# Row maxima of masked attention scores: the mask of half of the score banks is added by the vector engine instead of by a matmul

## The reference

```python
q, k, v = X @ Wq.T + bq, ctx @ Wk.T + bk, ctx @ Wv.T + bv      # 32 query heads of 8, 8 groups of keys and values
scores = einsum('bgrqd,bgkd->bgrqk', q, k) / sqrt(8)
scores = where(causal_mask | padding_mask, -inf, scores)
w = softmax(scores, axis=-1)
x = x + tanh(g_xattn) * ((w @ v) @ Wo.T + bo)                  # X is layernorm(x)
x = x + tanh(g_ffn) * moe(layernorm(x))                        # top 2 of 16 experts, silu(g) * u, 96 wide
```

## Time and profile before

| what | value |
|---|---|
| runs of the kernel before | 242.26 us, median of 3 (242.17 to 242.55) |
| the profiled execution, its own time | 242.28 us |
| its span, first to last instruction | 240.5 us |
| PE, DVE, ACT, POOL busy | 220.8, 170.2, 96.7, 94.8 us |

### The profile page before, as it was taken

The page is one execution under the profiler, slowest core; times in us unless marked ns, Lnnn a source line. Parts: engine busy times, 40 slices in busy tenths (PEclk is TensorE's granted clock), DMA queues, the critical chain, the costliest instruction groups (busy, mean ns, idle before and its releaser), DMA issues.

```text
span 240.5 us, 3821 instructions
## 1 busy us (share of the span) xinstructions
PE 220.8 (92%) x1279; PEld 159.1 (66%) x1279; DVE 170.2 (71%) x355; ACT 96.7 (40%) x190; POOL 94.8 (39%) x127
## 2 busy tenths in 40 slices
PE   0688798989999999999999899999999899999993
PEld 0675563565555555546466778879898798888892
DVE  2578978658777878785832678659984888774665
ACT  2456358756676767665776210110101111011000
POOL 6239325400608393937301021307996363320000
PEclk9999999999999999999999999999999999999998
DMA  6372320008761202020203100042546222123105
GB/s 186 102 235 57 78 55 22 4 0 180 170 149 29 60 8 67 1 65 9 59 8 131 46 0 0 5 140 64 147 114 189 94 87 81 52 46 88 44 0 174
DMA packets 26274, 18.33 MB, mean 76 GB/s; under 512 B 15600, under 2 KB 22320, under 8 KB 26256
## 3 DMA queue, kind: packets, MB, share of 16 engines
q1 hardware_dynamic: 25952, 17.87, 27.4%
q10 hardware_dynamic: 304, 0.22, 0.4%
HBM read 14.15 MB, written 1.11 MB: 63 GB/s over the span
## 4 chain that ended last, share of the span: by engine, by line
PE 70%; DVE 9%; POOL 7%; DMA 5%; ACT 3%; issue 3%; SPq 1%; ACTq 0%; DVEq 0%; POOLq 0%
PE bank L1019 64%; DMA wkv_n<-in_L_xattn_Wv 2%; DVE mneg L879 2%; POOL cT L551 2%; POOL w_d L555 2%; DMA w_t<-comb_d 2%; PE bank L1079 2%; POOL cT L550 2%; DVE pT L947 1%; POOL w_d L554 1%; ACT q L616 1%; DVE x_sb L1012 1%; DMA q<-q 1%; DVE q L953 1%; PE bank L1059 1%
## 5 line engine op out<-in xcount | busy, mean ns | idle before, releaser
L1019 PE MATMUL bank<-xT,cT 128*128 128x512 f32 x288 | 70.7, 393 | 1.0 <-DVE pT L939 0.7
L1019 PEld LDWEIGHTS bank<-xT,cT 128*128 128x128 f32 x288 | 52.6, 188 | 12.4 <-issue 1.2
L879 DVE TENSOR_REDUCE mneg<-bank 128x4 f32<-128x512 f32 x64 | 43.0, 684 | 11.6 <-PE bank L1019 10.6
L683 ACT ACTIVATE pT<-bank 128x512 f32<-128x512 f32 x24 | 14.4, 599 | 78.5 <-PE bank L1019 78.5
L696 ACT ACTIVATE pT<-bank 128x512 f32<-128x512 f32 x64 | 37.9, 599 | 18.8 <-PE bank L1019 17.8
L1019 PE MATMUL bank<-w_d,q 128*128 128x256 f32 x288 | 38.6, 284 | 1.7 <-issue 0.9
L1019 PEld LDWEIGHTS bank<-w_d,q 128*128 128x128 f32 x288 | 37.0, 190 | 4.5 <-issue 3.1
L1019 PE MATMUL bank<-q,kz 112*128 112x512 f32 x64 | 37.5, 586 | 0.0
L1019 PE MATMUL bank<-kz,q 96*128 96x512 f32 x64 | 26.5, 420 | 2.4 <-DVE mneg L879 1.8
L939 DVE TENSOR_TENSOR pT<-pT,bank 128x512 f32<-128x512 f32 x24 | 16.4, 684 | 17.1 <-PE bank L1019 15.2
L1019 PE MATMUL bank<-ident_b,cmask 128*128 128x512 bf16 x64 | 24.5, 383 | 1.2 <-ACT pT L696 0.6
(11 more groups left out here) (127 smaller groups left out, 278.3 us busy)
## 6 DMA issues: line engine op xcount, KB each, us to landing
w_t<-comb_d SPq DMA_DIRECT2D x16, 192.0 KB, 2.8
w_t<-comb_d SPq DMA_DIRECT2D x16, 128.0 KB, 2.9
padf<-in_L_ffn_down_w SPq DMA_DIRECT2D x12, 128.0 KB, 2.3
c_sb<-in_ctx SPq DMA_DIRECT2D x2, 512.0 KB, 6.5
q<-cT SPq DMA_DIRECT2D x8, 128.0 KB, 2.4
w_t<-comb_d SPq DMA_DIRECT2D x16, 64.0 KB, 2.7
out<-x_sb SPq DMA_DIRECT2D x4, 256.0 KB, 2.4
c_sb<-in_L_ffn_gate_w SPq DMA_DIRECT2D x8, 96.0 KB, 2.1
```

What stands on the lines that cost most here:

```text
L683: nc.scalar.activation(act_g[:, n % 2], bank[0][:], ACT.Silu).then_inc(a_ok, 1)
L879: nc.vector.tensor_reduce(mneg[:, r, 4 * hf:4 * hf + 4], bank[SQ_BANK[n % 3]][:].rearrange("p (g k) -> p g k", g=4), X, ALU.max, negate=Tr ...
L1019: return nc.tensor.matmul(dst, a, b, start=start, stop=stop, skip_group_check=True)
```

## The change

For the banks with odd `n` from 8 to 63 (half of the groups of batches 1 to 7, 28 banks) the mask matmul of the first pass goes. The matmul of queries and keys then ends the bank by itself and signals `s_done`. In its place `row_max` issues four fused operations on DVE, one for each group of 128 keys: each adds the scores in PSUM and `cmask` in SBUF, multiplies by -1, writes the 128 results to a new scratch tile `masked`, and keeps their minimum, which is the negated maximum, in `mneg`. The other 36 banks, and the whole second pass, are as before.

```diff
+        masked = sb("masked", [P, 4, L])
...
+        def added_by_reduction(n):
+
+            return bool(n % 2 and G <= n < CH)
...
             ve.wait_ge(s_done, n + 1)
             if n >= G:
                 ve.wait_ge(m_parts, n // G)
+            if added_by_reduction(n):
+                ve.wait_ge(max_ok, n - 1)
+                for g in range(4):
+                    ins = nc.vector.tensor_tensor_reduce(masked[:, g], bank[SQ_BANK[n % 3]][:, g * L:(g + 1) * L], cmask[:, n // G],
+                                                         -1.0, 4.0 * BIG, ALU.add, ALU.min, mneg[:, r, 4 * hf + g:4 * hf + g + 1])
+                ins.then_inc(max_ok, 1)
+                return
             nc.vector.tensor_reduce(mneg[:, r, 4 * hf:4 * hf + 4], ...
...
-            mm(ps[:], q4[...], kz[...], True, False)
+            bare = added_by_reduction(n)
+            ins = mm(ps[:], q4[...], kz[...], True, bare)
+            if bare:
+                ins.then_inc(s_done, 1)
+                return
             mm(ps[:], ident_b[:], cmask[:, b].unsqueeze(1).to_broadcast([P, 4, L]), False, True).then_inc(s_done, 1)
```

More of the change, by code:

```diff
@@ L1129, in scores_q @@
                 s, g4, ps = b % KZ, slice(4 * hf, 4 * hf + 4), bank[SQ_BANK[n % 3]]
-                mm(ps[:], q4[0:3 * QR, hf, r, toks(b)], kz[0:3 * QR, s, g4].rearrange("p g k -> p (g k)"), True, False)
+                bare = added_by_reduction(n)
+                ins = mm(ps[:], q4[0:3 * QR, hf, r, toks(b)], kz[0:3 * QR, s, g4].rearrange("p g k -> p (g k)"), True, bare)
+                if bare:
+                    ins.then_inc(s_done, 1)
+                    return
                 mm(ps[:], ident_b[:], cmask[:, b].unsqueeze(1).to_broadcast([P, 4, L]), False, True).then_inc(s_done, 1)
```

## The result

The changed kernel takes 240.29 us (median of 7 runs, 239.95 to 241.83) against 242.25 before (7 runs, 242.11 to 242.55). The ratio is 0.9925, 95% interval 0.9902 to 0.9947. The forecast was 243.0 us, slower; the measured time lies in its range, 239.0 to 253.0, and the direction is the other one, near rival 1's 239.8. The profiled execution took 239.97 us.

A forecast was written before the change was run, and what follows sets the result against it. PE bounds the kernel, and DVE takes over at nearly the same length. Opening +1.6, second piece -0.5, four full batches 0, last piece -0.4 sum to +0.7 us on 242.28: 243.0 us, range 239.0 to 253.0.

The forecast's parts named there:

- rival 1: POOL's stalls of `max_parts` go, up to 0.97 us a batch, and banks may cost less: 239.8 us; chance 0.28.
- PE's saving, 0.23 us a matmul: One mask matmul goes in each of 28 banks: 6.4 us in all on PE, 0.9 us a batch.
- PE alone would need only 10.5 us: Length of a full batch if PE alone bound it, against 11.4 to 11.6 us busy before.
- DVE's price of a bank, 1.12 us: Four overlapping pairs of fused operation and write replace a 0.60 us reduction: 0.52 us more a bank, 14.6 for 28.
- The opening, +1.6: Four banks before `max_parts` of batch 1: 2.1 us more on DVE, less its 0.48 us wait for ACT.
- Full batches even at 1.12 us a bank: Four full batches: DVE needs 2.1 us more where 1.9, 2.7, 2.1 and 2.1 are free, so 0 us.
- The 0.6 us of the second batch will be eaten: Second full batch: its -0.6 us is lost to waits that two engines near 100% give each other.
- the pairs under 0.25 us: Sign that the forecast is wrong: pairs of fused operation and write on DVE take under 0.25 us.
- the short `max_parts`: Sign of POOL's stalls going: `max_parts` short, beside batches of 10.5 to 10.9 us with PE still full.
- Rival 2: Fused operations on DVE don't overlap, 1.44 us a bank: +8.3 us, 250.6; chance 0.24, and 0.06 toward 1.77.
- Rival 3: POOL delays each of 112 fused operations by 0.138 us: 15 us more on DVE; chance 0.04.
- The clock stays at its upper level: PE's clock is granted as 1.00 also in pieces where PE has short waits.

The follow-up runs named there:

- pe_only: Changed kernel with the mask left out of the maxima of the 28 banks, so PE has its saving and DVE its old load; 238.8 us.
- from_batch2: Changed kernel with the change for the odd banks of batches 2 to 7 alone, 24 banks; 0.6 us faster than the changed kernel by the medians.
- bank_1_12_f2: Changed kernel with four one-column copies added to each fused bank, for batches 2 to 7 alone; at the upper end of 239.9 to 240.5 us.
- pool_pieces: Changed kernel with POOL's 512-column splits of the first four tiles' gate and up weights cut in four; within 0.4 us of the changed kernel.
- bank_1_12: Changed kernel with four idle one-column copies from PSUM added to each fused bank, which then takes 1.10 us; 242.93 us.
- all_from2: Changed kernel with all banks of batches 2 to 7 by fused operations and batch 1 the old way; 2.1 us below all_groups' median.
- all_groups: Changed kernel with all 56 banks of batches 1 to 7 by fused operations, two scratch tiles in turn; median 240.1 us.

## Why the prediction was wrong, step by step

- **PE's saving, 0.23 us a matmul: right.** Slots with a bare bank are 0.20 to 0.24 us shorter. With PE alone relieved (pe_only) the time falls by 3.4 us, of the 6.4 that 28 matmuls are worth. "PE alone would need only 10.5 us" a batch was wrong: it needs 10.71, because `TO` waits for ACT.
- **DVE's price of a bank, 1.12 us: wrong, and enough to turn the forecast's sign.** It measures 0.84, close to the lower end (0.82). I added 0.075 us for the write of each minimum, the pace of the shortest instructions; it costs almost nothing, since the next fused operation starts with it. The extra is 0.24 us a bank, 6.8 for all, and not 14.6. In the same sum, with 1.0 us more a batch where 1.9 to 2.7 are free, DVE is not the bound of the full batches: 0.5 - 0.5 - 4 x 0.9 - 0.4 is -4.0 us, 238.3. That is faster, and by 2 us too much: it lacks `TO`'s wait for ACT, in all four batches, and the wait behind POOL's stall, in two.
- **The opening, +1.6: right in kind, +0.74 in size.** By the same rule and the measured price it is 4 x 0.24 - 0.48 = 0.5. from_batch2 shows it from the other side: its opening is 0.72 us shorter.
- **Full batches even at 1.12 us a bank: wrong too.** bank_1_12_f2 has them 1.7 us shorter, -0.62, -0.67, -0.20 and -0.20. With this step right the forecast would have been 241.3 us, faster even at 1.12 us a bank. In the last two batches its picture nearly holds: DVE is busy for 10.92 of 11.18 us; its busy time grew by 1.9 us, not by 2.1. In the second its own arithmetic had given -0.6, and that came whole. In the first DVE's busy time grew by only 0.83 us (9.56 to 10.39), not by 2.1; that the engines run ahead of each other by up to three banks, so that a piece of DVE's work falls in another piece of the table, may be the reason, but no run shows it.
- **"The 0.6 us of the second batch will be eaten": wrong.** That piece has pe_only's length, 10.70 to 10.74 us, in every version with only the odd banks bare. The waits that were to eat it (PE can lead by three banks only) did not come.
- **Rival 1** had the time (239.8), and that was luck: it is the middle of two sums, both with a bank's cost too high (1.12 and 0.95 us) and with stalls that go. Its mechanism was wrong. `max_parts` did not leave POOL's way, because DVE's waits between the statistics and `max_parts` took up the added work, and PE's shorter slots drew it nearer (from 83.50, the aggregate, to 89.08 are 5.58 us, where it was 5.98 before), and the stalls grew. They cost 0.24 us in each of two batches (pool_pieces). Of its signs the pairs under 0.25 us and the full PE came, and the short `max_parts` did not.
- **Rival 2**, no overlap, 1.28 to 1.44 us a bank: excluded by the timeline. The estimate from the Trainium skill's figures (VectorE: DVE Perf Modes, the section on the TRN2 errata) was 1.28 us a bank, with 258 ns for an operation of 128 columns from PSUM. The trace does not agree: an operation takes 284 ns by its row, and the next one starts 211 ns after it. Another page of the Trainium skill (Vector Engine (DVE) Microarchitecture Reference, section 5.2) gives about 75 ns an instruction after overlap and 1.04 ns a column, from which I estimate 0.208 us for 128 columns. The trace agrees, 0.211, if the read of the accumulator is not counted as an instruction of its own.
- **Rival 3**, POOL blocks the fused operations: excluded. They take 258 to 292 ns throughout, 112 of them, with POOL busy beside them.
- **"The clock stays at its upper level": right for the changed kernel's profile, wrong as a rule.** The second pieces of pool_pieces and bank_1_12 show it down at 0.50 behind the longer wait in the opening. One of the changed kernel's seven runs took 241.83 us at a mean clock of 0.993, which may be the same; it left no trace, and runs of the kernel before at 0.991 took no longer than the others.

What was left out of the forecast altogether is the wait behind the next one: of the 0.89 us a batch that PE gives up, `TO` takes 0.22 back by waiting for ACT. ACT is 40% busy in the page, and this wait had not been looked for.

## What to carry to other kernels

Price a new instruction by the distance between starts where many follow each other, keep the lower end of that price as a full case, and ask which side of the other engine's slack it leaves you on: here the same sum gives 238.3 us with 0.84 us a bank and 243.0 with 1.12. When two engines are both near full, a stall that was free begins to cost: cutting POOL's instructions in four gave 0.0 us on the kernel before and 1.0 us on all_from2. And a run that hits the forecast number is not proof of it: cut the traces at the same events and compare the pieces.

## What the runs showed of the hardware that was not expected

- The read of a fused operation's result (82 ns by its row) is hidden behind the next fused operation: four pairs hold DVE for 0.84 us, four times the operation's own pace of 0.21.
- A wait of PE in the opening can cost twice: 0.82 us busy of 2 us in bank_1_12, and then a granted clock of 0.82, 0.50 and 0.83 over 6 us, and a next piece 1.5 to 1.7 us longer. In pool_pieces' profile (17.20 against 15.73 us) it followed a wait of 1.5 us, with which other profiles kept 1.00. all_groups' profile kept 1.00 even with a wait of 2.02 us and PE busy for 0.87 of the same 2 us. So the wait does not bring the clock down each time, and what decides is not shown.
- What POOL runs beside it decides the time of `max_parts`' cast from SBUF to SBUF: it takes 181 ns free, 0.23 us beside the end of a memset, and up to 1.19 us in the changed kernel beside an instruction of 512 columns. Beside a memset too it ends only when POOL's instruction has ended.
